# A fused two-block decoder layer: expert rows added into DRAM by accumulating DMAs, and a later place for the next block's keys and values

## What is computed

```python
h = _rms(x, ff_ln_w)                      # 1024 tokens x 512, after the self attention
weights = ...                             # softmax over the top 4 of 16 expert logits, else 0
y = silu(h @ w1[e]) * (h @ w3[e]) @ w2[e] # for each of the 16 experts
moe = jnp.einsum('bsed,bse->bsd', y, weights)
return x + moe
# third part: keys and values of 2 x 1024 context rows, keys with a layer norm per head
k = _ln(kv[..., :HD], kn_w, kn_b)
```

## Time and profile before

| what | value |
|---|---|
| median of the runs (lowest to highest) | 2946.0 us (2941.17 to 2949.18), 3 runs |
| the profiled execution, time | 2944.19 us |
| its span | 2942.4 us |
| busy: PE, DVE, ACT, POOL | 2398.4, 1768.0, 1472.8, 1100.9 us |
| norm with steps of keys and values | 1556.0 to 1614.8 us |
| routing | 1614.8 to 1650.7 us |
| rest of keys and values | 1650.7 to 1711.6 us |
| experts | 1711.6 to 2190.2 us |
| combination | 2190.2 to 2264.6 us |

### The profile page before, as it was taken

The page is one execution under the profiler, slowest core; times in us unless marked ns, Lnnn a source line. Parts: engine busy times, 40 slices in busy tenths (PEclk is TensorE's granted clock), DMA queues, the critical chain, the costliest instruction groups (busy, mean ns, idle before and its releaser), DMA issues. The chain is left out here.

```text
span 2942.4 us, 46079 instructions
## 1 busy us (share of the span) xinstructions
PE 2398.4 (82%) x14790; PEld 1995.1 (68%) x14790; DVE 1768.0 (60%) x3807; ACT 1472.8 (50%) x3030; POOL 1100.9 (37%) x1497
## 2 busy tenths in 40 slices
PE   5999999999957998899885649889860689999355
PEld 3778787878756888888873548888860577777232
DVE  3555555555554666666666625454535688888576
ACT  3444444444435666666653533333320587777543
POOL 0222222232313444444442555565633454444000
PEclk9999999999987999999996869999985799999788
DMA  3000000000010000000004654545546224241100
GB/s 108 19 17 12 7 18 11 18 7 18 0 29 11 19 18 18 18 18 18 18 1 136 207 171 168 174 161 170 169 130 177 79 61 108 61 107 65 75 8 22
DMA packets 124097, 194.94 MB, mean 66 GB/s; under 512 B 18736, under 2 KB 67120, under 8 KB 122224
## 3 DMA queue, kind: packets, MB, share of 16 engines
q1 hardware_dynamic: 109312, 157.50, 17.6%
q0 software_dynamic: 6640, 21.76, 2.3%
q10 hardware_dynamic: 8064, 14.68, 1.4%
HBM read 149.87 MB, written 44.04 MB: 66 GB/s over the span
## 5 line engine op out<-in xcount | busy, mean ns | idle before, releaser
L435 ACT ACTIVATE x_p<-x_p,x_least 128x1024 f32<-128x1024 f32 x128 | 147.3, 1151 | 307.3 <-DVE x_least L391 307.3
L1812 POOL TENSOR_TENSOR e_w<-e_raw,e_w 128x2048 fp32r<-128x2048 f32 x48 | 220.4, 4593 | 154.5 <-ACT e_w L1778 154.4
L375 DVE TENSOR_TENSOR x_pT<-pair,x_pT 128x512 fp32r<-128x512 f32 x256 | 164.3, 683 | 122.3 <-ACT x_pT L454 122.3
L469 POOL TENSOR_TENSOR x_carry<-x_rtotal 128x1 f32<-128x1 f32 x128 | 24.7, 193 | 559.8 <-DVE x_rtotal L368 559.8
L2143 PE MATMUL pair<-m_h,e_w 128*128 128x320 f32 x1536 | 230.5, 311 | 2.4 <-POOL e_w L1812 2.4
L2143 PEld LDWEIGHTS pair<-m_h,e_w 128*128 128x128 f32 x1536 | 229.0, 190 | 4.2 <-issue 2.8
L537 PE MATMUL pair<-x_pT,x_v 128*128 128x256 f32 x1536 | 209.5, 293 | 9.2 <-DVE x_pT L375 9.2
L537 PEld LDWEIGHTS pair<-x_pT,x_v 128*128 128x128 f32 x1536 | 193.9, 194 | 26.3 <-issue 18.3
L565 PE MATMUL pair<-x_kT,x_qT 128*128 128x512 f32 x768 | 206.9, 404 | 0.0
L993 ACT ACTIVATE s_p<-s_p,s_least 128x128 f32<-128x128 f32 (+3 forms) x256 | 143.6, 561 | 123.1 <-DVE s_least L903 122.9
L1131 PE MATMUL pair<-s_pT,s_v 128*128 128x256 f32 (+1 forms) x1152 | 158.8, 284 | 47.3 <-DVE s_pT L880 47.3
(11 more groups left out here) (337 smaller groups left out, 6079.6 us busy)
## 6 DMA issues: line engine op xcount, KB each, us to landing
e_raw<-in_L_ffn_w SPq DMA_DIRECT2D x48, 1024.0 KB
z_v<-z_vst SPq DMA_DIRECT2D x16, 768.0 KB, 3.4
y_rows<-hslot ACTq DMA_DIRECT2D x48, 256.0 KB, 4.7
z_kS<-z_k SPq DMA_DIRECT2D x24, 512.0 KB, 9.3
z_vS<-z_v SPq DMA_DIRECT2D x8, 1536.0 KB, 6.7
f_raw<-in_L_ffn_w SPq DMA_DIRECT2D x2, 4096.0 KB, 13.2
z_qS<-z_q SPq DMA_DIRECT2D x24, 256.0 KB, 4.2
s_wraw<-in_L_ffn_wq SPq DMA_DIRECT2D x9, 512.0 KB, 4.3
```

The lines of the kernel that those rows point to most:

```text
L375: dve.tensor_tensor(pT[1][:, keys, q * P:(q + 1) * P], TR[j][:, :].rearrange("p (k n) -> p k n", n=P), pT[0][:, keys, q * P:(q + 1) * P].b ...
L435: act.activation(p[n][:, :], p[n][:, :], ACT.Exp, scale=-1.0, bias=least[:, n:n + 1], accum_out=total[:, n:n + 1]).then_inc(s_ex, 1)
L1812: pool.tensor_tensor(dst[1][:, :, :], raw[parity][:, :, :], dst[0][:, :, :].bitcast(F32), ALU.subtract).then_inc(s_lo, 1)
```

## The change

`y_rows`, `where`, `share` by token and the combination go. SP stores `y` to a DRAM tensor `y_sum` before the routing. The list that PE makes for an expert has six columns in place of two: the token number in two parts, a one for a filled place, and the token's weight in three bf16 parts. DVE makes a target row for every place from it (the token's row, or an own dummy row behind the tokens for an empty place), multiplies each output block by the weights while it copies it from PSUM, and POOL adds it to `y_sum` by an indirect DMA that accumulates. Each of the 48 such DMAs waits until the one before has landed. At the end SP loads `y_sum` back into `y` in two halves.

```diff
-        RMS_FIRST = 3
-        kv_place = {"rms": range(0, NT - RMS_FIRST), "turned": range(5, 6), "picked": range(6, 7), "gated": range(7, 8), "after": range(8, 22)}
+        RMS_FIRST = 6
+        kv_place = {"rms": range(0, NT - RMS_FIRST), "turned": range(2, 4), "picked": range(4, 6), "gated": range(6, 7), "after": range(7, 22)}
...
-                        if t < RMS_FIRST:
-                            kv["ACT0"](act, 2 * t)
-                            kv["ACT0"](act, 2 * t + 1)
-                        else:
+                        if RMS_FIRST - 3 <= t < RMS_FIRST:
+                            kv["ACT0"](act, 2 * (t - RMS_FIRST + 3))
+                            kv["ACT0"](act, 2 * (t - RMS_FIRST + 3) + 1)
+                        elif t >= RMS_FIRST:
...
-                        if rows and t in (1, RMS_FIRST):
+                        if rows and t in (RMS_FIRST - 2, RMS_FIRST):
...
+                u = s - TLAG - 1
+                if B <= u < len(units) and (u - B) % 2:
+                    n = u - B
+                    dve.wait_ge(s_fh, u + 1)
+                    if n >= 2:
+                        dve.wait_ge(s_st[1], 16 * 2 * (n // 2))
+                    dve.tensor_tensor(stlo[1][:, :, :], tt[u % 2][:, :, :], sthi[1][:, :, :].bitcast(F32), ALU.subtract).then_inc(s_fl2, 1)
...
-                    if B <= u < len(units):
+                    if B <= u < len(units) and (u - B) % 2 == 0:
...
             def sync(sp):
+                sp.dma_start(y_sum[0:T, :].rearrange("(t p) d -> p t d", p=P), y3).then_inc(s_ysum, 16)
...
-                step(dve.tensor_copy(token[:, :, :], token32[:, :, :]))
+                token = moe["token"]
+                step(dve.memset(token[:, NE:, :, 3:], 0.0))
+                step(dve.tensor_copy(token[:, :, :, 0:3], token32[:, :, :].unsqueeze(1).to_broadcast([P, NE + 2, NT, 3])))
+                step(dve.tensor_copy(token[:, 0:NE, :, 3], gate[:, :, :]))
+                step(dve.tensor_tensor(left[:, :, :], gate[:, :, :], token[:, 0:NE, :, 3], ALU.subtract))
+                step(dve.tensor_copy(token[:, 0:NE, :, 4], left[:, :, :]))
+                step(dve.tensor_tensor(left[:, :, :], left[:, :, :], token[:, 0:NE, :, 4], ALU.subtract))
+                step(dve.tensor_copy(token[:, 0:NE, :, 5], left[:, :, :]))
...
-                step(dve.tensor_tensor(row[:, :, :], placed, first[:, :].unsqueeze(1).to_broadcast([P, NT, NE]), ALU.add))
-
-                src = chosen
-                for k in range(4):
-                    n, dst = 1 << k, rank[k % 2]
-                    step(dve.tensor_copy(dst[:, :, 0:n], src[:, :, 0:n]))
-                    step(dve.tensor_tensor(dst[:, :, n:], src[:, :, n:], src[:, :, 0:NE - n], ALU.add))
-                    src = dst
-                step(dve.tensor_tensor(rank[0][:, :, :], src[:, :, :], chosen[:, :, :], ALU.mult))
-                for k in range(TOPK):
-                    for value, dst in ((row[:, :, :], row_k), (by_token, share)):
-                        step(dve.scalar_tensor_tensor(pick[:, :, :], rank[0][:, :, :], k + 1.0, value, ALU.is_equal, ALU.mult))
-                        step(dve.tensor_reduce(dst[:, k, :], pick[:, :, :], AX.X, ALU.add))
-                step(dve.tensor_copy(where[:, :, :], row_k[:, :, :]))
...
+                sp.wait_ge(s_sum, 16 * CT * NE)
+                for k in range(2):
+                    sp.dma_start(y3[:, k * NT // 2:(k + 1) * NT // 2, :],
+                                 y_sum[k * T // 2:(k + 1) * T // 2, :].rearrange("(t p) d -> p t d", p=P)).then_inc(s_back[k], 16)
...
+                def scatter(e, s, r):
+
+                    pool.wait_ge(s_yd, CT * (e + 1) + r + 1)
+                    pool.wait_ge(s_tg, TARGET * (e + 1))
+                    if not (isinstance(e, int) and e == 0 and r == 0):
+                        pool.wait_ge(s_sum, 16 * (CT * e + r))
+                    n = 52 + CT * s + r
+                    pool.tensor_tensor(scrap[:, n:n + 1], eps[:, 0:1], eps[:, 0:1], ALU.mult)
+                    pool.indirect_dma_start(y_sum, bass.IndirectOffsetOnAxis(ap=target[s][:, r:r + 1], axis=0),
+                                            y3[:, CT * s + r, :], None, compute_op=ALU.add).then_inc(s_sum, 16)
...
+                def body(i, s, first, last):
                     e = i * 2 + s
                     gather(e + 1, 1 - s)
+                    if not first:
+                        scatter(e - 1, 1 - s, 0)
                     low(pool, w2, 3 * e + 3, s)
+                    if not first:
+                        scatter(e - 1, 1 - s, 1)
                     if not last:
                         low(pool, w1[1 - s], 3 * e + 4, (3 * s + 1) % 2)
+                    if not first:
+                        scatter(e - 1, 1 - s, 2)
+                    if not last:
                         low(pool, w3[1 - s], 3 * e + 5, (3 * s + 2) % 2)
...
+                def targets(e, s):
+
+                    dve.wait_ge(s_id, LIST * e + 1)
+                    if not (isinstance(e, int) and e < 2):
+                        dve.wait_ge(s_sum, 16 * CT * (e - 1))
+                    dve.tensor_reduce(share[s][:, :], lists[s][:, :, 3:6], AX.X, ALU.add).then_inc(s_tg, 1)
+                    dve.tensor_reduce(target32[0][:, :], lists[s][:, :, 0:2], AX.X, ALU.add).then_inc(s_tg, 1)
+                    dve.tensor_tensor(target32[1][:, :], lists[s][:, :, 2], dummy[:, :], ALU.mult).then_inc(s_tg, 1)
...
                         mark(e + 2, range(m * NT // HC, (m + 1) * NT // HC))
+                    targets(e, s)
                     part_low(HC - 1)
...
-                        dve.wait_ge(s_st[k], (CT * 16) * i + 16 * ((CT * s + r) // 2 + (0 if k == (CT * s + r) % 2 else 1)) + 16)
-                        dve.tensor_copy(hslot[:, k * D:(k + 1) * D], Y[(r + 1) % 2][:, :]).then_inc(s_yd, 1)
+                        dve.tensor_scalar(y3[:, CT * s + r, :], Y[(r + 1) % 2][:, :], share[s][:, r:r + 1], None, ALU.mult).then_inc(s_yd, 1)
...
-                            mm = pe.matmul(Y[0][:, 2 * r:2 * r + 2], mine[:, t, r * P:(r + 1) * P], token[:, t, :],
+                            tok = moe["token"][:, e, t, :] if isinstance(e, int) else (
+                                moe["token"][:, bass.ds(e, 1), t, :].rearrange("p e k -> p (e k)"))
+                            mm = pe.matmul(Y[0][:, 6 * r:6 * r + 6], mine[:, t, r * P:(r + 1) * P], tok,
                                            start=(t == 0), stop=(t == NT - 1))
```

More of the change, by code:

```diff
@@ L1933, in tokens, with body @@
                         act.activation(XS[s][0][:, c, :], TR[c % 2][:, 0:CAP], ACT.Copy).then_inc(s_xh, 1)
-                def store(e, s, r):
-                    act.wait_ge(s_yd, CT * (e + 1) + r + 1)
-                    k = (CT * s + r) % 2
-                    row = e * PLACES + r * P
-                    dst = y_rows[row:row + P, :] if isinstance(e, int) else y_rows[bass.ds(row, P), :]
-                    act.dma_start(dst, hslot[:, k * D:(k + 1) * D]).then_inc(s_st[k], 16)
                 tokens(0, 0)
-                def body(i, s, first, last):
+                def body(i, s, last):
                     e = i * 2 + s
@@ L1957, in body @@
                     high(act, w2[0], 16 * (3 * i + (1 if s == 0 else 3)) + (0 if s else 16), s)
-                    if not first:
-                        store(e - 1, 1 - s, CT - 1)
                     for m in range(HC):
@@ L2061, in few_vector @@
                 dve.wait_ge(s_up, 16)
+                dve.wait_ge(s_ysum, 16)
                 mark(0)
```

124 lines of the change are left out of this document (59 added, 65 removed).

## The result

Changed kernel 2956.7 us (median of 6 runs, 2955.0 to 2958.8), kernel before 2944.9 (2940.5 to 2949.2): ratio 1.0046, 95% interval 1.0034 to 1.0057. The change made the kernel slower by some 12 us, where 39 less were forecast. The profiled execution has a span of 2953.2 us, 10.8 more than before's 2942.4.

A forecast was written before the change was run, and what follows sets the result against it. Three places were taken to count: the tail, PE's queue in the experts, and the chain before them. -55 + 1 + 16 + 4 - 5.5 + 0.3 = -39 us, giving 2907 against the median 2946.0; range 2882 to 2940.

The forecast's parts named there:

- The tail: Behind the last expert: only three accumulating DMAs, the reload of `y` and `add_inner` remain; -55 us.
- A doubled landing: Accumulating DMAs landing in 7.4 us: the chain would still fit and the tail alone lose 7 us.
- The 1 us for `wqraw`: Next stage's first needed load, queued behind the reload of `y`, would land about 1 us late at most.
- 0.3 us as a bound: PE's `order` in the experts: 0.3 us longer per expert if each of the 8 addresses is made once.
- three more experts at 1.5, +4: Experts: a longer thin stretch on PE makes the clock fall in three more experts, 1.5 us each, +4.
- the upper bound of 12 us: Experts: upper end of the 0 to 12 us given for more frequent clock falls.
- Rival B: Experts: `order` takes 3.0 us, clock drops in 8 more experts; experts +48, total 2935; chance 0.15.
- One cover: DVE in the experts: `targets` adds 1 to 1.5 us, covered before PE needs the low part; zero or +0.3 an expert.
- Before the experts: Norm, routing and rest of keys and values, with the stage moved: -5.5 us in sum (-13 to +6).
- Its low parts come later, at about 1596: Norm: POOL's weight low parts come later, but fewer tiles and steps remain; logits at 1608.5, -6.3 us.
- -4: Behind the routing: halving POOL's low parts of the keys saves 0.25 us in 9 steps, 0.6 in three.
- Rival D: Before the experts: POOL's late weights and DVE's waits for ACT make it 8 us longer; total 2920; chance 0.08.

The follow-up runs named there:

- before_reg: Kernel before, with only `order` reading its token columns at a loop-register address, no scatter, `targets` or moved stage: 2985.2 us against 2944.4.
- dyn_fold: padded without the conversion of row numbers (the reduction writes the integer tile), `order` keeping its register addresses: 2939.9 us against padded's 2937.9.
- static: padded with `order`'s right-hand side at a fixed address, VectorE copying the expert's token columns into a small tile: 2925.0 us.
- static_fold: static without the conversion of row numbers, the reduction from PSUM writing the integer tile directly: 2905.6 us, experts 456.4.
- old_place: padded with only the places of the key and value stage as in the kernel before: 2924.4 us, part before the experts 177.3.
- no_half: padded with only the keys' low parts all back on POOL, places as in the change: 2937.8 us.
- padded: Changed kernel plus never-run VectorE and ScalarE instructions, so the second cross attention's loop begins where before, modulo 128 instructions: 2937.9 us.
- dyn_busy: dyn_fold with 16 unread transposes on PE ahead of its wait for the marks: 2913.3 us, experts 465.8.
- best_busy: static_fold with keys and values as in the kernel before, plus 16 unread transposes on PE ahead of its wait for the marks: 2872.8 us, 0.9759.

## Why the prediction was wrong

Forecast and result lie some 51 us apart. By the table at the head, 20 of them are in the experts, 15.5 before them and 18 in the second cross attention; the tail was 2 us better than forecast.

**The tail was right.** Sums 5.6 us apart (5.7 taken), landing 4.7 to 4.9 us after issue (5.2), `add_inner` 18.3 us behind the last copy (19), -56.8 (-55). A doubled landing, the 7.4 us that the prediction worked out beside the Trainium skill (Collectives: The Full Stack, "The bandwidth ceiling: the fold count and why AG ≠ RS ≠ AR"), did not come. The 1 us for `wqraw` did not show.

**The experts' mechanism was right, its size was not.** `order` became 0.77 us longer (1.0 taken), and the clock dipped more often, as said. The 0.77 is partly luck: not 24 addresses are made but 8, for which the prediction had 0.3 us as a bound. The step that failed is "three more experts at 1.5, +4": the dip came in 8 more experts, in all 16, and deeper, and cost 24 to 26 us, of which the first 12 products by w2 alone show 20 (58.9 us over all experts before, 78.9 after). I priced the clock per dip, and took the number of dips as nearly fixed, where the kernel already stood at the edge: in the earlier trace rows one expert has the dip and the one ahead of it has not, with the same gap. What a longer thin stretch does there could not be read from the trace, and the upper bound of 12 us was a guess without a row. Rival B had the sum of the experts nearly (+48), through an `order` of 3.0 us that did not come.

**One cover was priced at nothing and named wrongly.** For `targets` I looked at PE's wait for the low part and found it covered; that it delays the conversion past the start of POOL's operation, some 4 us of DVE in place of 0.2, I did not see. The longer `order` alone does the same: in before_reg, without `targets`, the conversion begins 0.6 us behind POOL's operation and takes 4.0. In the changed kernel this cost nothing, since the slow clock covered it (dyn_fold). It cost 19 us as soon as `order` was short again (static against static_fold).

**Before the experts the sign was wrong.** Routing came as worked out (35.9 to 37.0 us), by luck, as two errors go against each other: the operations on the token tile added 5 us and not 2.2 (a subtraction of 128 elements a row took 1.16 us and, two operations later, 0.33), and two steps cost 5.7 us (old_place) and not 7.4. Wrong were two steps. "Its low parts come later, at about 1596": the first product came at 1605.39, behind waits of 5.3 and 5.8 us of DVE for stores of `hslot` in tiles 2 and 4 and of 13.7 us of PE for the rows, so that the shorter remainder gained nothing: the norm took 59.5 us from 1556.5 on, in place of 58.8, where 6.3 less were forecast. And "-4" for the halved low parts: the steps behind the routing came every 4.3 us in place of 3.9, in no_half every 4.0, and no_half shows that the half gains nothing. What follows the routing took 93.3 us in place of 85.2, 8.1 more, where the forecast's terms sum to nothing; the places account for 5.8 of them (padded against old_place). Rival D had this part (+8 against +10.0).

**The loop's code was not in it at all.** 18 us, half again as much as the total result, have nothing to do with what the change computes. Without them the changed kernel takes 2937.9 (padded), faster than before by 0.2%, inside the range that was given, but by the tail alone; the other steps failed all the same.

The four parts of the table sum to +11.9, the spans differ by 10.8; the other 1 lies between them. The rivals were set up as alternatives, each with the rest of the forecast unchanged; B's sum for the experts and D's for the part before them came together. With both, the forecast would have been -39 + 28 + 13.5 = +2.5, and with the measured sizes it is -56.8 + 40.4 + 10.0 = -6.4, which is what padded shows (-7.8).

## What to carry to other kernels

Before a change's arithmetic is believed, compare the code's place: where a loop's body is some 300 instructions long, as here, look at the first instruction behind each jump back for idle time put down to "issue" and count the instruction packets; dead code ahead of the loop moves it at no cost. On VectorE, ask of each small conversion, copy or two-input operation between SBUF tiles which long GpSimd operation runs beside it and which starts first; a conversion folded into a reduction from PSUM escapes. Keep a matmul's operand address free of loop registers by copying the slice to a fixed tile, and if PE has a gap ahead of a dense stretch, try to fill it.

## What the runs showed of the hardware

- A jump back to loop code that has to be loaded again: 7.3 to 8.1 us of idle time on the engine, 8 to 9 us of the kernel, 10 more packets of 8 KB on q14 for one engine and 19 for two, over two jumps.
- A conversion of 3 numbers a row on VectorE took 0.17 us alone and 3.9 to 4.6 us beside a GpSimd operation of 4.6, 9.08 beside two in a row; a subtraction of two SBUF tiles of 320 columns 0.48 and up to 3.2; a reduction from PSUM 0.15 us in both cases.
- A register in the address of a 6-column or a 2-column moving operand: 24 matmuls 1.45 to 1.52 us in place of 0.75 to 0.81, also in dyn_busy, where the clock was at its upper level during all 16 of the loop.
- An accumulating indirect DMA of 128 rows of 2 KB into DRAM: issue 1.56 to 1.66 us on POOL (a gather 0.95 to 1.0), 4.7 to 4.9 us from issue to landing behind the experts, 6.5 in the median of all 48, most of them beside the experts' loads (changed kernel).
- 16 idle transposes (1.9 us) in a gap of 2.8 us kept PE's clock at the upper level in all 16 experts of best_busy, and in 8 of 16 in dyn_busy, whose `order` behind them is 0.7 us longer. Why exactly the clock falls, and in which experts, was not settled further.
